# Softmax maxima by VectorE and DMA, keys staged in parts, four PSUM banks for two pairs of scores and two for units

## The reference

```python
q = (x @ wq).reshape(b, n, heads, dh).transpose(0, 2, 1, 3)
k = (ctx @ wk).reshape(b, j, heads, dh).transpose(0, 2, 1, 3)
v = (ctx @ wv).reshape(b, j, heads, dh).transpose(0, 2, 1, 3)
sim = jnp.einsum('bhid,bhjd->bhij', q, k) * scale
a = jax.nn.softmax(sim, axis=-1)
out = jnp.einsum('bhij,bhjd->bhid', a, v)
...
a, g = jnp.split(h3 @ ff_w1 + ff_b1, 2, axis=-1)
ff = a * jax.nn.gelu(g, approximate=False) @ ff_w2 + ff_b2
```

## Time and profile before

| what | value |
|---|---|
| median of 3 runs | 3690.73 us (3683.37 to 3697.74) |
| the profiled execution's own time | 3690.11 us |
| its span | 3688.3 us |
| PE busy | 3235.1 us, 88% |
| DVE busy | 2080.8 us, 56% |
| ACT busy | 1989.5 us, 54% |
| POOL busy | 620.7 us, 17% |
| granted TensorE clock, mean | 0.931 |

### The profile page before, as it was taken

One profiled execution on the slowest core, in us unless ns is written; L12 is line 12 of the kernel. 1 busy time (PEld: TensorE's weight loads), 2 busy tenths in 40 slices (PEclk: granted clock), 3 DMA queues, 4 the chain that ended last, 5 costly groups with the idle time before them and its releaser, 6 DMA issues.

```text
span 3688.3 us, 43767 instructions
## 1 busy us (share of the span) xinstructions
PE 3235.1 (88%) x16320; PEld 1493.1 (40%) x16320; DVE 2080.8 (56%) x2565; ACT 1989.5 (54%) x3806; POOL 620.7 (17%) x676
## 2 busy tenths in 40 slices
PE   5887888998899989999899988999988988887877
PEld 2333333343353434534344433544344534433435
DVE  5555565665555765557555655556755665455511
ACT  1543565656655656456664566545665566354531
POOL 2231121203102120112202132021210031001001
PEclk8987988999998999999999888999999999998989
DMA  6434335333433243332443445323333243222202
GB/s 156 140 90 97 95 89 141 89 82 88 126 89 108 68 107 94 95 96 53 130 107 87 120 119 147 97 90 72 92 92 87 46 101 90 63 43 47 69 24 71
DMA packets 194515, 340.88 MB, mean 92 GB/s; under 512 B 19384, under 2 KB 101696, under 8 KB 193024
## 3 DMA queue, kind: packets, MB, share of 16 engines
q1 hardware_dynamic: 194304, 338.08, 35.5%
HBM read 202.29 MB, written 114.75 MB: 86 GB/s over the span
## 4 chain that ended last, share of the span: by engine, by line
PE 60%; DVE 14%; DMA 11%; ACT 6%; POOL 3%; issue 3%; SPq 3%; DVEq 0%; ACTq 0%; POOLq 0%
DVE mx L933 12%; PE pr L1124 11%; PE po L1141 11%; PE pd L1105 7%; PE pf L1049 5%; PE pf L996 5%; PE pf L1060 5%; DMA QS<-scr_q 5%; PE pf L1019 3%; PE pf L1037 3%; ACT ET L852 3%; PE pf L1028 3%; DMA scr_k<-HS 2%; PE pf L1052 2%; DMA raw<-ff_w_dram 1%
## 5 line engine op out<-in xcount | busy, mean ns | idle before, releaser
L852 ACT ACTIVATE ET<-pr 128x512 f32<-128x512 f32 (+1 forms) x2720 | 1478.1, 596 | 1372.5 <-PE pr L1124 1356.8
L933 DVE TENSOR_REDUCE mx<-pd 128x2 f32<-128x804 f32 (+2 forms) x1600 | 1569.4, 1033 | 1004.2 <-PE pd L1105 1001.7
L1124 PE MATMUL pr<-QS,KS 64*128 64x512 f32 (+1 forms) x2720 | 871.0, 514 | 86.6 <-ACT ET L852 84.1
L1105 PE MATMUL pd<-KS,QS 64*128 64x400 f32 (+2 forms) x3200 | 636.2, 396 | 160.0 <-DVE mx L933 85.4
L1141 PE MATMUL po<-ET,V 128*32 128x512 f32 (+2 forms) x5440 | 770.2, 640 | 1.2 <-ACT OU L858 1.2
L1124 PEld LDWEIGHTS pr<-QS,KS 64*128 64x128 f32 (+1 forms) x2720 | 337.4, 189 | 962.7 <-ACT ET L852 648.5
L1105 PEld LDWEIGHTS pd<-KS,QS 64*128 64x128 f32 x3200 | 361.1, 197 | 302.9 <-DVE mx L933 194.0
L743 POOL TENSOR_TENSOR HS<-uT,HS 128x512 fp32r<-128x512 f32 (+4 forms) x168 | 189.9, 1131 | 762.5 <-ACT uT L816 762.5
L759 POOL TENSOR_TENSOR OA<-OA,DEN 128x512 f32<-128x512 f32 (+1 forms) x48 | 60.8, 1267 | 1259.5 <-DVE DEN L941 1259.5
L1049 PE MATMUL pf<-HS,WS 128*128 128x512 f32 x730 | 217.7, 430 | 50.1 <-DVE uT L926 17.8
L1019 PE MATMUL pf<-cT,w_kv 96*128 96x400 f32 (+3 forms) x384 | 168.3, 564 | 31.5 <-ACT uT L816 30.6
(11 more groups left out here) (82 smaller groups left out, 2186.0 us busy)
## 6 DMA issues: line engine op xcount, KB each, us to landing
WS<-parts SPq DMA_DIRECT2D x160, 320.0 KB, 2.9
KS<-scr_k SPq DMA_DIRECT2D x80, 600.8 KB, 10.6
QS<-scr_q SPq DMA_DIRECT2D x80, 512.0 KB, 10.2
scr_k<-HS SPq DMA_DIRECT2D x144, 200.0 KB
scr_q<-HS SPq DMA_DIRECT2D x96, 256.0 KB
KS<-scr_k SPq DMA_DIRECT2D x80, 192.0 KB, 3.7
scr_k<-HS SPq DMA_DIRECT2D x48, 256.0 KB
OA<-OU SPq DMA_DIRECT2D x320, 32.0 KB
```

What stands on the lines that cost most here:

```text
L852: activation(ET[0:q.rows[k], s % 2, 2 * pair + e, :], pr[e][0:q.rows[k], :], ACT.Exp).then_inc(score_free, 1)
L933: v.reduce_max(mx[:, t, 2 * p:2 * p + 2, c], pd[no % 2][:, :, 0:cols], AX_X).then_inc(unit_free, 1)
L1105: ins = mm(pd[no % 2][:, e, 0:cols], queries[:, t * P:(t + 1) * P], keys, start=True, stop=True)
L1124: mm(pr[e][0:m, :], keys, queries, start=True, stop=True).then_inc(score_ready, 1)
```

## The change

1. The two pd buffers become one pd of two banks, and pr[0] and pr[1] become buffers of two banks, one for each pair of heads. Both matmuls of a pair signal once, and ScalarE takes one exponential of 1024 columns instead of two of 512. A unit waits for the reduction of the unit before it.
2. The turning by TensorE and the four copies into QS go. VectorE copies the two parts of the maxima into MS (now 32 columns), transposes it in four blocks of 32 partitions into MT, and SyncE writes MT into the query rows with two DMAs (`put_maxima`), which the first scores of a group wait for.
3. Staging is split into queries (slots by SLOTS, one semaphore each) and keys, and the keys of a C group into two parts (HALVES) that are loaded as soon as their columns are free (`read_until`). Units of a C group go chunk by chunk, so that the first half needs the first part alone.
4. Units get places by a model of the time of each beat (FILL_LENGTH, AT): one at even beats and, inside fills of 1.5 or more of that model, one in the middle (three inside ff2), between the fill's matmuls (`between`). LATE goes.
5. Fills are dealt a little differently: v2a and n1 in the mixed phases, ff2 of the last but one phase moved into the last one, fewer beats from a group's end to its reciprocals and division in the two first phases (INVERT_ALONE, DIVIDE_ALONE).

The core of the diff:

```diff
-         "C": [(p, q, c, n, cols) for p in range(HG // 2) for q in range(TT) for c, (n, cols) in enumerate(CHUNKS)]}
+         "C": [(p, q, c, n, cols) for c, (n, cols) in enumerate(CHUNKS) for p in range(HG // 2) for q in range(TT)]}
+
+HALVES = {"S": [(0, T)], "C": [(0, CHUNKS[2][0]), (CHUNKS[2][0], JP)]}
...
+    def read_until(self, first, last):
+
+        steps = [k for k in range(self.kt) if self.at + k * P < last and first < self.at + k * P + self.rows[k]]
+        return self.step0 + steps[-1] + 1 if steps else 0
+
...
+            _own = [p.slot for p in GROUPS if p.kind == _kind and (_kind == "C" or p.step0 >= 2 * G * TT)]
+            if _kind == "C" and _crosses >= 2 and _i is not None:
+                _slot = _own[-2]
+            elif len(GROUPS) == 2 * G - 1:
+
+                _slot = GROUPS[-2].slot
+            elif _kind == "S" and _own:
+                _slot = _own[-1]
+            else:
+                _slot = min(_last, key=_last.get)
...
+def read_until(q, part):
+
+    if part < 0:
+        return max([p.end for p in GROUPS[:q.n] if p.slot == q.slot], default=0)
+    first, last = HALVES[q.kind][part]
+    return max([p.read_until(q.at + first, q.at + last) for p in GROUPS[:q.n]], default=0)
...
+STAGED_IN = {"S": 6.0, "C": 8.0}
+LAST_UNIT_AHEAD, PUT_BEHIND = 6.0, 3.0
...
+    for b in range(BEATS):
+        length = sum(FILL_LENGTH.get(p[0], 0.0) for p in PLACES.get(b, []))
+        if b % 2 == 0:
+            yield b, AT[b]
+        elif b % 4 == 1 and fills_at(b) == 1 and length >= 1.5:
+            count = 1 + int(length > 3.0) * 2
+            for k in range(count):
+                yield b, AT[b] + length * (k + 1) / (count + 1)
...
+    _rate, _need, _sum = 0.0, 0, 0
+    for _n in sorted(n for n in _left if _left[n]):
+        _sum += units_now(_n, _now)
+        _rate = max(_rate, _sum / max(UNITS_TO[_n] - _now, 0.5))
+        _need = max(_need, -(-_sum // max((4 * GROUPS[_n].step0 - 1 - _b) // 2, 1)))
+    _credit = min(max(_credit + _rate * (_now - _before), _need), max(_need, 2))
+    _before = _now
+    for _ in range(int(_credit >= 1.0) if _b % 2 else max(_need, int(_credit >= 1.0))):
+        _n = next((n for n in sorted(_left) if _left[n] and units_now(n, _now)), None)
+        if _n is None:
+            break
+        UNITS_AT[_b].append((_n, len(GROUPS[_n].units) - _left[_n]))
+        _left[_n] -= 1
+        _credit -= 1.0
+        if not _left[_n]:
+            assert _b < 4 * GROUPS[_n].step0
+            PUT_AT.setdefault(min(beat_at(_now + PUT_BEHIND), 4 * GROUPS[_n].step0 - 1), []).append(GROUPS[_n])
...
-        pd = [es.enter_context(nc.psum_tensor(f"pd{i}", [P, 2, 512], F32)) for i in range(2)]
-        pr = [es.enter_context(nc.psum_tensor(f"pr{i}", [P, 512], F32)) for i in range(2)]
+
+        pd = es.enter_context(nc.psum_tensor("pd", [P, 2, 512], F32))
+        pr = [es.enter_context(nc.psum_tensor(f"pr{i}", [P, 2, 512], F32)) for i in range(2)]
...
-                sp.dma_start(QS[:, q.ring, :, :].bitcast(F32), qs.rearrange("(p e) r n -> (e r) p n", e=2)
-                             ).then_inc(staged[q.ring], 16)
+                    sp.dma_start(KS[ROWS * e + ROWS - DATA:ROWS * e + ROWS, :, q.at + first:q.at + last].bitcast(F32),
+                                 rows[:, e, :, first:last].rearrange("p r n -> r p n")).then_inc(keys_in[q.kind, q.at, part], 16)
+
+            def put_maxima(q):
+                sp.wait_ge(max_steps, MAX_STEPS * (q.n + 1))
+                for e in range(2):
+                    row = QS[ROWS * e:ROWS * e + 2, q.slot, :, :].rearrange("r p (t n) -> r (p t) n", n=P)
+                    sp.dma_start(row.bitcast(F32), MT[HG * TT * e:HG * TT * (e + 1), q.n % 2, :].bitcast(F32)
+                                 ).then_inc(max_in[q.n % 2], 16)
...
-                for e in range(2):
-                    act.wait_ge(score_ready, HG * s + 2 * pair + e + 1)
-                    activation(ET[0:q.rows[k], s % 2, 2 * pair + e, :], pr[e][0:q.rows[k], :], ACT.Exp).then_inc(score_free, 1)
+                act.wait_ge(score_ready, 2 * s + pair + 1)
+                activation(ET[0:q.rows[k], s % 2, 2 * pair:2 * pair + 2, :], pr[pair][0:q.rows[k], :, :], ACT.Exp
+                           ).then_inc(score_free, 1)
...
-            def place_maxima(q):
-                act.wait_ge(turned, q.n + 1)
-                for e in range(2):
-                    copy(QS[ROWS * e:ROWS * e + 2, q.ring, 0, :], pd[0][32 * e:32 * e + 2, 0, :]).then_inc(max_copied, 1)
...
+            def minus_maxima(q, no):
+                dve.wait_ge(unit_free, no + 1)
+                v.tensor_reduce(nm[:, :, :], mx[q.kind][:, :, :, :], AX_X, ALU.max, negate=True).then_inc(max_steps, 1)
+                dve.wait_ge(max_steps, MAX_STEPS * q.n + 1)
+                by_head = nm[:, :, :].rearrange("q t (p e) -> q e p t", e=2)
+                high, low = MS[:, :, 0, :, :], MS[:, :, 1, :, :]
+                v.tensor_copy(high, by_head).then_inc(max_steps, 1)
+                dve.wait_ge(max_steps, MAX_STEPS * q.n + 2)
+                v.tensor_tensor(low, by_head, high.bitcast(F32), ALU.subtract).then_inc(max_steps, 1)
+                if q.n >= 2:
+                    dve.wait_ge(max_in[q.n % 2], 32 * (q.n // 2))
+                dve.wait_ge(max_steps, MAX_STEPS * q.n + 3)
+                for b in range(0, P, 32):
+                    columns = MS[b:b + 32, :, :, :, :].rearrange("q e s p t -> q (e s p t)")
+                    v.transpose(MT[:, q.n % 2, b:b + 32].bitcast(F32), columns.bitcast(F32)).then_inc(max_steps, 1)
...
-                if no >= 2:
-                    pe.wait_ge(unit_free, no - 1)
+                if no >= 1:
+                    pe.wait_ge(unit_free, no)
...
+                no = 2 * s + pair
+                if no >= 2:
+                    pe.wait_ge(score_free, no - 1)
...
-                    mm(pr[e][0:m, :], keys, queries, start=True, stop=True).then_inc(score_ready, 1)
+                    ins = mm(pr[pair][0:m, e, :], keys, queries, start=True, stop=True)
+                ins.then_inc(score_ready, 1)
```

More of the change, by code:

```diff
@@ L277 @@
 TAIL = FILL["o2", N - 1, 0]
[L280 to L293, removed]
-for _q in GROUPS:
[L295 to L310, removed]
-    TURN_AT[_beats[-1] + _lag] = _q
-    _free = _beats[-1] + _lag + 2
@@ L313, with split_for @@
-UNITS_BEFORE = [len(GROUPS[0].units) + sum(UNITS_AT[:b]) for b in range(BEATS)]
-assert sum(UNITS_AT) + len(GROUPS[0].units) == len(UNIT)
-ENDED = {4 * q.end: q for q in GROUPS}
-def ended(beat, behind):
-    return ENDED.get(beat - behind)
-def ended_slot(beat, behind):
-    q = ended(beat, behind)
+def split_for(q, part):
+    own = ("q" if part < 0 else "k") + ("1" if q.kind == "S" else "2")
+    if own != "k2":
+        return own, q.i, q.g // 2
+    return own, q.i, len(CHUNKS) * (q.g // 2) + 2 * part + 1
@@ new lines, in units_now, with unit_places @@
+def units_now(n, now):
+    q = GROUPS[n]
+    parts = len(HALVES[q.kind])
+    staged = sum(UNITS_FROM[n, part] <= now for part in range(parts))
+    return max(staged * len(q.units) // parts - (len(q.units) - _left[n]), 0)
+UNITS_AT, PUT_AT = {b: [] for b in range(BEATS)}, {}
+def unit_places():
+    for b in range(BEATS):
[6 more added lines that the diff above has]
+                yield b, AT[b] + length * (k + 1) / (count + 1)
@@ new lines, with ended @@
+assert not any(_left.values())
+UNIT = [(0, u) for u in range(len(GROUPS[0].units))]
+UNITS_BEFORE = []
+for _b in range(BEATS):
+    UNITS_BEFORE.append(len(UNIT))
+    UNIT += UNITS_AT[_b]
+assert len(UNIT) == len(set(UNIT)) == sum(len(q.units) for q in GROUPS)
+_through = [n for n, u in UNIT if u == len(GROUPS[n].units) - 1]
+assert _through == sorted(_through)
+ENDED = {4 * q.end: q for q in GROUPS}
+def ended(beat, behind, behind_alone):
+    for q, count in ((ENDED.get(beat - behind), behind), (ENDED.get(beat - behind_alone), behind_alone)):
+        if q and count == (behind_alone if q.end <= 2 * G * TT else behind):
+            return q
+    return None
@@ L326, in ended_slot @@
+def ended_slot(beat, behind, behind_alone):
+    q = ended(beat, behind, behind_alone)
     return q if q and (q.g % 2 or q.g == G - 1) else None
@@ L331, in slots_before @@
     return KC * q.i + q.g // 2
-def fills_at(beat):
-    return sum(p[0] in STAGE for p in PLACES.get(beat, []))
-LATE = {b for b in PLACES if 0 <= b < BEATS and b % 4 == 1 and fills_at(b) < 2 and not fills_at(b + 2)}
 def repeated(a, rows, row, times):
@@ L961, in _ @@
             for beat in range(FIRST_BEAT, BEATS + BEATS_BEHIND + 1):
+                if 0 <= beat < BEATS and beat % 2:
+                    for no in range(UNITS_BEFORE[beat], UNITS_BEFORE[beat] + len(UNITS_AT[beat])):
+                        reduce(no)
                 for p in PLACES.get(beat, []):
```

283 lines of the change are left out of this document (158 added, 125 removed).

## The result

The changed kernel takes **3906.48 us** (median of 4 runs, 3903.49 to 3913.86), the kernel before 3691.19 beside it: ratio 1.0587 (95% interval 1.0562 to 1.0613), 5.9% slower. The prediction was 3575, range 3400 to 3710: wrong in sign. Rival 2, with 3840, named the wait that grew, though not its pattern; that its number came near is partly luck (see why the prediction was wrong).

A forecast was written before the change was run, and what follows sets the result against it. The prediction took TensorE's in-order queue, with its waits for others, as the bound. Savings of -369 us and additions of +255 gave -114 from 3690, 3576, taken as 3575 us, range 3400 to 3710.

The forecast's parts named there:

- Rival 2: At unit_free: the single pair of unit banks becomes the bound once the mean round trip passes 1.67 us; 3840, chance 0.15.
- (b): A unit's round trip from start to end of its reduction, 1.42 us with the signal, not hidden inside fills: +60 us.
- (c): VectorE's other work, such as reciprocals and additions, stands directly in TensorE's way without a second unit buffer: +75 us.
- the scores: With two banks for each pair, TensorE's pairs of scores mostly stop waiting for ScalarE's exponentials: -238 of 278 us.
- the maxima's DMA: At group starts: maxima sent by DMA land late for some of the 80 groups, 0.75 us each: +60, ends 0 and 240.
- The clock: Granted clock, 0.77 in the stretch with blocked stores: the prediction took back nothing for it.
- Rival 4: Waits inside busy pairs of scores were no loss and stay, -369 becoming -180: 3690 to 3760 us, chance 0.07.
- (a): Units on TensorE standing alone, no longer second of two at a beat, cost more: +60 us, ends 0 and 150.
- staging: Queries and keys staged in parts: units' 71.5 us of waiting for DMA shrink to some 10, -61 us.
- the turning: L1111's 320 matmuls leave TensorE's queue, 48.1 us busy and 2.5 idle: taken as -45 us.
- the exponentials: ScalarE's one exponential of 1024 columns for each pair, x1360, expected at about 1.03 us.
- the blocked stores: Key stores stuck in SyncE's queue behind staging, with ScalarE waiting for their buffers (24.5 us, line 813): -25 us.

The follow-up runs named there:

- e10: Changed kernel with each of its 192 reciprocals over 8 columns instead of a quarter of the sums: 3825.79 us, ratio 1.0360.
- e9: Changed kernel with each of its 1600 reductions over 8 columns of each head instead of 400 or 512: 3479.32 us, ratio 0.9417.
- e1: Changed kernel with units at even beats alone, none inside fills: 4216.63 us, ratio 1.1428.
- e8: Kernel before with the new banks alone, its plan of two units at an even beat kept: 4796.0 us, ratio 1.2988.
- e3: Changed kernel with ScalarE taking a group's sums ahead of the fill of the same beat, not behind it: 3870.53 us, ratio 1.0498.
- e12: Changed kernel with the banks of before, sums ahead of the fill, and no units in k2 fills: 3638.13 us, ratio 0.9841.
- e2: Changed kernel with the banks of before and exponentials of 512 columns, everything else as changed: 3693.35 us, ratio 1.0002.
- e6: Changed kernel with the banks of before and the sums taken ahead of the fill: 3658.47 us, ratio 0.9898.
- e4: Changed kernel with one reduction for each head's bank, the next unit's first matmul waiting for the first bank alone: 3944.47 us, ratio 1.0675.
- e11: Changed kernel with the banks of before, sums ahead of the fill, and units due two steps earlier in the plan: 3666.42 us, ratio 0.9913.
- e5: Changed kernel with the banks of before and units at even beats alone: 3836.48 us, ratio 1.0376.
- e7: Changed kernel with the banks of before, units at even beats alone, and sums ahead of the fill: 3801.34 us, ratio 1.0283.

## Why the prediction was wrong

**The step that failed is the pricing of the single pair of unit banks**, terms (b) and (c), +135 in all. Measured, the units' wait for reductions rose from 85.4 to 328.8, +243 us (all idle time before units is 356). Group by group, the units came to +294 where the terms for them give 60 + 60 + 75 - 61 = +134, the weighing to +91 where nothing stood, and the scores with the maxima's DMA to -145 against -238 + 60 = -178. The three together are 284 of the 330 us between 3906 and 3576; groups overlap, so this is rough.

- *A term left out.* "A unit is placed at every even beat" was taken as one unit to a beat. The plan that the change makes has 76 even beats with two and 10 with three, where fills are short; a unit behind another waits nearly a whole round trip, 142 us in all (79 before, when pairs at one beat had two buffers). The plan is arithmetic on constants of the kernel and could have been counted before.
- *(b), 60*: the round trip behind scores and fills is 88 + 28 = 116, some 24 of it DMA and issue, so about 92. The 1.42 us was right for an undisturbed unit of 400 columns (1.43), but the mean is 1.63. For units of 512 keys it is 1.72 (937.29 to 939.01), which the term did not use though they are a fifth of the units.
- *(c), 75*: by the table 61 + 37 = 98; e10 gives 81 for the reciprocals alone. Right in size, at the low side.
- *The clock.* The prediction let it stand. It fell from 0.931 to 0.905: 233 us more at 1.2 GHz, in which TensorE does half, so up to 117 us. e9 shows it come back with most of the waits gone, e1 and e8 (0.860, 0.825) show it fall further with more of them. Rival 2's 0.25 for each unit was too much as a mean wait (356 / 1600 = 0.22) and yet gave 66 us too little in time, since it had neither this nor the sums, and stood on savings that came out smaller. That 3840 is near 3906 is partly luck.
- *Rival 2's threshold.* It was said to decide from a mean round trip of 1.67 us. The loss was there although the measured mean is 1.63: the spacing of the units is not even, and a mean says nothing of the 110 that stand directly behind another one.

**What was not seen at all:** LATE's removal, to which the prediction gives no term. It puts ScalarE's copy of the sums behind a fill: weighing +91 (72 of it waiting), 36 us in time (e3).

**The scores**, -238 forecast, measured -145. The -145 has the 31.8 of the maxima's DMA in it, which the forecast counts elsewhere; without them it is -177. The mechanism was right: the pairs start with their banks free (idle on exponentials 84.1 to 14.5), and each is busy 765.6 / 1360 = 0.56. Of the 278 us a part was no wait for a bank but the lower clock, where a pair takes 0.79 instead of 0.50. By the trace 219 of the 2720 matmuls started at the lower clock before, 290 after: an estimate of 110 x 0.29 = 32 us that stayed, and grew to 42. Rival 4 was thus right in a small part.

**(a) Units alone**, 60 forecast with ends 0 and 150: the units are busy 94 us more. Some 20 of that is the clock by the same estimate (432 matmuls of units started at the lower one, 290 before). The k2 step puts it at 0.06 for each unit, and shows what the term had named and not priced: the split fill, 0.27. e12's 20 us go in this direction, if they are more than noise.

**Right, with one exception:** staging, -61 forecast, -63 measured in the units' wait; the turning, -45 against 50.6; the exponentials at 1024 ns; the maxima's DMA, where +60 was taken and the scores wait 31.8. The -25 for the blocked stores did not come: ScalarE waits 57 us for such stores now (lines 938 and 943), 48 before (lines 808 and 813).

The Trainium skill (ScalarE: Activation LUTs, What ACT_TABLE_LOAD costs) gives, as an estimate, 1.04 us for 1024 columns; these runs have 1.024. Its rule in Perfetto Trace Analysis, Matmuls, that independent matmul groups should rotate through PSUM banks, was cited as speaking against this part; e2 sizes what giving up that rotation for the units cost here, 213 us net of what the scores gained.

**What stays open:** how the 213 us divide between idle time and clock (only bounds are given above), and why all parts but the banks are worth nothing together in e2: the saved waits for DMA and the turning stand against the sums (35 us, e6) and the pieces, but the rest of that balance was not taken apart. Staging, the maxima by DMA and the plan of the units were never tried one without the other.

## What to carry to other kernels

When a buffer moves from one producer to another, price both by the round trip from the writer's start to its release, for the pairs of users that really follow each other: run the plan by hand and count them, since the mean spacing hides those that stand back to back. If TensorE already waits in one place, ask what the clock does there: in two steps with a new wait of 1.3 us at each even beat the granted clock was 0.61, and the work around the waits took 1.6 to 1.8 times as long. A split that relieves one queue by loading a single serial chain (here 1600 trips of 1.4 us in 3700) has to be tried by itself, apart from the edits that come with it: the same edits with the banks of before, and the sums ahead of the fill, beat the kernel before by 1.0% (e6), and by 1.6% without units in k2 fills (e12).

## What the runs showed of the hardware

- A second instruction is not free: two reductions of 400 columns take 2 x 0.567 (e4), one of 800 takes 0.99; 16 columns take 0.171 (e9). ScalarE's two exponentials of 512 columns take 2 x 0.596, one of 1024 takes 1.024: 97 us less busy for the whole kernel. No run shows that this by itself shortened anything.
- A transposition of a block of 32 by 32 by VectorE takes 0.200 us (x320, 64.1 us).
- Between two parts of one accumulation matmuls into other banks can be put (the k2 step above); the fill in two parts took 1.81 instead of 1.54 us, besides the matmul between.
- TensorE's clock was lower where it waited more, but no single wait gives the order. By the units' waits for VectorE: 0.944 (e9, 63.2 us), 0.940 (e2, 65.1), 0.931 (before, 85.4), 0.905 (after, 328.8), 0.860 (e1, 468.9), 0.825 (e8, 860.3). Against this order stand e11 with 0.946 at 97.9, e5 with 0.905 at 99.1 (its scores wait 218.9 for the maxima) and e4 with 0.900 at 176.2 (its units wait between their matmuls too). By all idle time of TensorE the order is closer: 344 to 378 us at 0.940 to 0.946 (e12, e6, e11, e9, e2), 453 at 0.931, 502 to 608 at 0.903 to 0.916 (e7, e5, e10, e3, after), 892 at 0.860, 1144 at 0.825; e4 (460 at 0.900) stays out.
